# Layer 3 of a four-layer mixture-of-experts kernel: extra work moved inside a tile's slot, on ScalarE in front of the rounding, on TensorE in front of the down products

## The reference, cut to what matters

```python
# the conditioned part, for each chosen expert and the shared one
g = x @ gate_w;  u = x @ up_w
x1 = sum_e w_e * (gelu(g, approximate=True) * u) @ down_w
# the layer's own part
h   = rmsnorm(x1) * gamma1
q   = (h @ Wq + bq).reshape(b, t, 16, 16)
kv  = ((h @ Wdown + bdown) @ Wup + bup).reshape(b, t, 16, 32)   # k, v
att = softmax(einsum('bthd,btgd->bthg', q, k) / 4)              # heads against heads of one token
x2  = x1 + einsum('bthg,btgd->bthd', att, v).reshape(b, t, 256) @ Wo + bo
gate = softmax(rmsnorm(x2) * gamma2 @ Wg + bg)
out  = x_in + x2 + einsum('btd,edf,bte->btf', h2, We, gate)
```

## Time and profile before

| | us |
|---|---|
| median of 3 runs | 1460.94 (1460.05 to 1464.66) |
| the profiled execution | 1467.98 |
| its span | 1465.3 |
| TensorE busy (matmul) | 1292.0 (88%) |
| VectorE busy | 1017.1 (69%) |
| GpSimd busy | 628.9 (43%) |
| ScalarE busy | 573.3 (39%) |

### The profile page before, as it was taken

The page is one execution under the profiler, slowest core; times in us unless marked ns, Lnnn a source line. Parts: engine busy times, 40 slices in busy tenths (PEclk is TensorE's granted clock), DMA queues, the critical chain, the costliest instruction groups (busy, mean ns, idle before and its releaser), DMA issues.

```text
span 1465.3 us, 18770 instructions
## 1 busy us (share of the span) xinstructions
PE 1292.0 (88%) x6536; PEld 1093.1 (75%) x6536; DVE 1017.1 (69%) x1854; ACT 573.3 (39%) x960; POOL 628.9 (43%) x339
## 2 busy tenths in 40 slices
PE   5998999998992899838888999999899989996798
PEld 4898687897791799826677787877678777875687
DVE  8699777599662555546766433489748994799986
ACT  3401423303320688714445454434443344432242
POOL 4320115620015567573303462375445442565691
PEclk9899999899975899969999999999899999998799
DMA  6310002310007689851101647323213161232000
GB/s 193 145 37 15 29 19 82 132 29 1 0 15 254 206 274 315 264 172 43 44 0 35 223 169 250 127 73 126 111 50 109 50 244 65 73 122 101 0 1 29
DMA packets 45885, 154.96 MB, mean 106 GB/s; under 512 B 6992, under 2 KB 7776, under 8 KB 45664
## 3 DMA queue, kind: packets, MB, share of 16 engines
q1 hardware_dynamic: 38848, 136.08, 27.7%
q0 software_dynamic: 4608, 12.59, 2.6%
q10 hardware_dynamic: 2336, 5.11, 0.9%
HBM read 120.98 MB, written 32.77 MB: 105 GB/s over the span
## 4 chain that ended last, share of the span: by engine, by line
PE 57%; DVE 22%; issue 9%; POOL 5%; ACT 4%; DMA 2%; SPq 1%; DVEq 0%; ACTq 0%; POOLq 0%
PE bank L442 17%; PE bank L446 16%; PE bank L445 16%; DVE G L498 3%; DVE bank L2472 3%; DVE acc L2496 2%; DVE F L2496 2%; POOL w_lo L679 1%; POOL VW L498 1%; PE bank L1056 1%; PE bank L1228 1%; POOL xs L687 1%; PE bank L1373 1%; DVE acc L2628 1%; PE bank L928 1%
## 5 line engine op out<-in xcount | busy, mean ns | idle before, releaser
L442 PE MATMUL bank<-x_hi,w_hi 128*128 128x512 f32 (+1 forms) x560 | 218.6, 390 | 27.9 <-POOL w_lo L725 6.3
L445 PE MATMUL bank<-x_lo,w_hi 128*128 128x512 f32 (+1 forms) x560 | 212.6, 380 | 0.0
L446 PE MATMUL bank<-x_hi,w_lo 128*128 128x512 f32 (+1 forms) x560 | 212.2, 379 | 0.0
L725 POOL TENSOR_TENSOR w_lo<-raw,w_hi 128x1024 fp32r<-128x1024 f32 x36 | 89.4, 2482 | 196.1 <-ACT w_hi L1718 181.9
L442 PE MATMUL bank<-hid_hi,w_hi 128*128 128x512 f32 x328 | 133.3, 406 | 22.6 <-DVE hid_lo L2427 12.3
L442 PEld LDWEIGHTS bank<-x_hi,w_hi 128*128 128x128 f32 x560 | 110.2, 197 | 54.5 <-issue 18.5
L1819 ACT ACTIVATE hid_hi<-bank 128x512 fp32r<-128x512 f32 x96 | 57.6, 600 | 215.1 <-DVE bank L2472 215.1
L445 PE MATMUL bank<-hid_lo,w_hi 128*128 128x512 f32 x328 | 131.2, 400 | 0.0
L446 PE MATMUL bank<-hid_hi,w_lo 128*128 128x512 f32 x328 | 130.8, 399 | 0.0
L446 PEld LDWEIGHTS bank<-x_hi,w_lo 128*128 128x128 f32 x560 | 109.7, 196 | 19.2
L445 PEld LDWEIGHTS bank<-x_lo,w_hi 128*128 128x128 f32 x560 | 110.2, 197 | 17.8
(11 more groups left out here) (468 smaller groups left out, 3537.1 us busy)
## 6 DMA issues: line engine op xcount, KB each, us to landing
raw<-in_skill SPq DMA_DIRECT2D x32, 768.0 KB
raw<-in_l1e SPq DMA_DIRECT2D x20, 513.0 KB
base<-xs SPq DMA_DIRECT2D x38, 256.0 KB, 4.4
ys<-F SPq DMA_DIRECT2D x38, 256.0 KB, 4.8
VW<-in_l1e SPq DMA_DIRECT2D x18, 513.0 KB, 5.3
w_hi<-kept SPq DMA_DIRECT2D x12, 768.0 KB, 4.3
w_lo<-kept SPq DMA_DIRECT2D x12, 768.0 KB, 6.1
raw<-in_l0c SPq DMA_DIRECT2D x12, 512.0 KB
```

What stands on the lines that cost most here:

```text
L442: i = nc.tensor.matmul(out, sh, mh, start=first, stop=False)
L445: nc.tensor.matmul(out, sh, ml, start=False, stop=False)
L446: return nc.tensor.matmul(out, sl, mh, start=False, stop=last)
L725: nc.gpsimd.tensor_tensor(lo[:, UP3], src[:, UP3], hi[:, UP3].bitcast(F32), ALU.subtract).then_inc(w_up_ready.sem, 1)
```

## The change

ScalarE: a new place between a tile's gelu and its rounding. `dense_hi` of rounds 2 to 4 goes there from behind the rounding. The four passes for the norm (squares and copies, L1744 and L1746) go there from in front of the gelu of slot 2, and into slot 1. The rounding of the transposed attention output (`o3_hi`, L1777) goes there from in front of gelu, in slot 5.

TensorE: a new place between up and down products. The sums of squares (slot 2), the second pair of queries (slot 8), keys and values 1 (slot 9), the transposes (slot 5 instead of 4) and the first of two expert products of one slot (slots 13, 14, 15, 16, 18 and 20) go there. What else these functions did stays where it was. The order of VectorE, GpSimd and SyncE, the tail's order and the buffers stay too.

```diff
-            def attention3(q, i, x, y):
+            def attention3_between(q, i, x, y):
                 w = q % 2
                 if i == 2:
                     pe.wait_ge(*sq1(q, 2))
                     pe.wait_ge(*base_ready(q, 2))
                     norm_stats(x, w).then_inc(ss1.sem, 1)
+                if i == 8:
+                    pe.wait_ge(*lat_lo(q, 1))
+                    pe.wait_ge(lat_pad.sem, 3)
+                    queries(w, 1, x)
+                if i == 9:
+                    pe.wait_ge(*q3_sb(q, 2))
+                    keys_values(1, x)
...
-            def finish3(p, i, x, y):
+            def finish3_between(p, i, x, y):
                 w, last = p % 2, p == BATCH - 1
-                if i == 4:
+                if i == 5:
                     pe.wait_ge(*sum_dve(p, 16))
                     pe.wait_ge(*sum_pool(p, 16))
                     pe.wait_ge(*(x_final(1, 2) if last else n3_F(p + 1, 2)))
...
+                for j in range(1, 16):
+                    if WE_SLOT[j - 1] != i and WE_SLOT[j:j + 2] == [i, i]:
+                        experts3(p, j, (x, y)[j % 2])
...
                 for j in range(16):
-                    if WE_SLOT[j] == i:
+                    if WE_SLOT[j] == i and WE_SLOT[j:j + 2] != [i, i]:
                         experts3(p, j, (x, y)[j % 2])
...
                     l3_up(b, i)
+                    if 0 <= q:
+                        attention3_between(q, i, x, y)
+                    if 0 <= p:
+                        finish3_between(p, i, x, y)
                     if g >= 2:
                         l3_down(g - 2)
...
-            def attention3_before(q, i, x, y):
+            def attention3_between(q, i, x, y):
                 w = q % 2
-                if i == 2:
+                if i == 1:
                     act.wait_ge(*d3_step(q, TILES3))
...
                         nc.scalar.activation(gelu3[g % 2], PB[g % 2][0][:], ACT.Gelu_apprx_tanh).then_inc(g3_gelu.sem, 1)
+                    if 0 <= q < BATCH:
+                        attention3_between(q, i, x, y)
+                    if 0 <= p < BATCH:
+                        finish3_between(p, i, x, y)
+                    if next_chunk and b > 0:
+                        dense_hi(n)
+                    if b < BATCH:
                         act.wait_ge(*g3_gated(0, g + 1))
...
                         nc.scalar.activation(hid_hi[0][:, g % HID3, :], PB[g % 2][1][:], ACT.Copy).then_inc(g3_hi.sem, 1)
-                    if next_chunk and b > 0:
-                        dense_hi(n)
```

More of the change, by code:

```diff
@@ L1250, in attention3 @@
                     norm_stats(x, w).then_inc(ss1.sem, 1)
+                if i == 8:
[5 more added lines that the diff above has]
+                    keys_values(1, x)
+            def attention3(q, i, x, y):
+                w = q % 2
                 if i == 3:
@@ L1268, in attention3 @@
                 if i == 8:
-                    pe.wait_ge(*lat_lo(q, 1))
-                    pe.wait_ge(lat_pad.sem, 3)
-                    queries(w, 1, x)
                     pe.wait_ge(*q3_sb(q, 1))
@@ L1274, in attention3 @@
                 if i == 9:
-                    pe.wait_ge(*q3_sb(q, 2))
-                    keys_values(1, x)
                     pe.wait_ge(*kv3_sb(q, 1))
@@ L1292, in finish3 @@
                         mm.then_inc(o3T_ready.sem, 1)
+                for j in range(1, 16):
+                    if WE_SLOT[j - 1] != i and WE_SLOT[j:j + 2] == [i, i]:
+                        experts3(p, j, (x, y)[j % 2])
+            def finish3(p, i, x, y):
+                w, last = p % 2, p == BATCH - 1
                 if i == 6:
@@ L1429, in _ @@
             l3_down(TILES3 * BATCH - 1)
-            attention3(LQ, 2, att_x, att_y)
+            attention3_between(LQ, 2, att_x, att_y)
             attention3(LQ, 3, att_x, att_y)
@@ L1746, in attention3_before @@
                         nc.scalar.activation(base[w][:, m, :], (x, y)[m][:], ACT.Copy).then_inc(base_ready.sem, 1)
+            def attention3_before(q, i, x, y):
+                w = q % 2
                 if i == 3:
@@ L1777, in finish3_before @@
                         nc.scalar.activation(h_hi[w][:, m, :], (x, y)[m][:], ACT.Copy).then_inc(o3_hi.sem, 1)
+            def finish3_before(p, i, x, y):
+                w = p % 2
                 if i == 11:
@@ L1868, in gate_exps @@
                 nc.scalar.activation(p, logits, ACT.Exp).then_inc(l3_exp.sem, 1)
-            attention3_before(LQ, 2, mlp_x, mlp_y)
+            attention3_between(LQ, 1, mlp_x, mlp_y)
             attention3_before(LQ, 3, att_x, att_y)
@@ L1879, in _ @@
             keys_values_out(LQ, 3, mlp_x)
-            finish3_before(LP, 5, *out_bank)
+            finish3_between(LP, 5, *out_bank)
             finish3_after(LP, 7)
```

2 lines of the change are left out of this document (1 added, 1 removed).

## The result

The changed kernel takes 1469.91 us (median of 11 runs, 1466.46 to 1473.88), the kernel before beside it on the same chip 1459.27 us (11 runs, 1454.8 to 1464.66): ratio 1.0076, 95% interval [1.0058, 1.0094], or +11.1 us. The forecast was +6.1 us and slower; the sign was right and the size short by 5 us.

The account below looks back on a forecast made before the run. TensorE, nearly full on average, has the last word in slots 3 to 11, VectorE from slot 12 to the next round's slot 2. 8.2 - 4.3 - 1.4 + 3.6 + 0 = +6.1 us on 1460.94 gives 1467.0 us, range 1458.5 to 1474.

Parts of the forecast that it names:

- Slots 8 and 9: Rounds 2 to 4: queries, keys and values wait uncovered for VectorE, down products come on top; 1.36 us per slot, +8.2 us.
- Norm and transposes, round 3: Slots 1 to 5: earlier norm passes and later transposes remove TensorE waits; -4.3 us with a new low-clock stretch, -5.9 without.
- The same, round 4: Transposes' wait goes, saving 2.2 us, norm gains 0; with an even chance of a low-clock stretch, -1.4 us.
- Weights' rounding: Slots 12 to 18, rounds 3 and 4: earlier GpSimd residue makes VectorE's products wait longer; +1.8 us a round, +3.6 us.
- the walk through slot 12: Rounds 3 and 4: stepping through durations, VectorE's product waits about 1.4 us in slot 12; 5.9 us over slots 12 to 18.
- Round 2, 0: Round 2: GpSimd's work and VectorE's products fill the port before and after, so the earlier weights' rounding changes nothing, 0 us.
- Experts' order: Slots 13 to 20: first expert product before the down products is just covered; 0, up to 1 us a round if lead gone.
- 1 (relief): Rounds 3 and 4: GpSimd's residue ends before VectorE's product, 8.3 us of waits vanish; -5.8 us, 1455.1 us, chance 0.12.
- 2: Whole kernel: gains cancel losses, no new low-clock stretches and port as today; +0.1 us, 1461 us, chance 0.20.
- rival 3: Slots 8, 9, 3 and experts' firsts: new waits bring low-clock stretches, experts' lead used up; about +12, 1473 us, chance 0.13.

Follow-up runs that it names:

- queries_back: Changed kernel with the second queries and keys and values 1 put back behind the down products; ratio to the kernel before 1.0040, loop +5.9 us.
- gains_only: Kernel before with only the norm's passes and sums of squares and the transposes moved; ratio to before 0.9970, loop -5.5 us.
- slot12_only: gains_only plus the early weights' rounding in slot 12 of rounds 3 and 4 alone; ratio to before 1.0050, loop +0.6 us.
- pool_order: gains_only with GpSimd's head product before L725 in slots 12 to 17 of rounds 3 and 4, behind VectorE's in odd slots; ratio to before 1.0027.
- small_reduced: slot12_only with the gate's two small products turned into one-input reductions, its weights' normalisation left out; ratio to before 0.9971, loop -4.9 us.
- gains_round2: gains_only plus the early weights' rounding in round 2 from slot 12 on; ratios to before 0.9968 and, run again, 0.9960.
- dense_back: Changed kernel with the weights' rounding put back behind the tile's rounding; ratio to before 1.0025, loop -1.8 us.
- experts_back: Changed kernel with both expert products of a slot put back behind the down products; ratio to before 1.0091, loop +4.8 us.
- slot12_back: Changed kernel with the weights' rounding of slot 12 of rounds 3 and 4 alone put back; ratio to before 1.0012, loop -4.5 us.
- after_reduced: Changed kernel with the gate's two small products turned into reductions, its weights' normalisation left out; ratio to before 1.0034, loop 0.0 us.

## Why the prediction was right on the sign and short on the size

- **Slots 8 and 9, +8.2 us: right.** 8.15 measured, 1.36 each, with the idle times and releasers named (1.49 and 1.44 us, forecast about 1.6 and 1.5). queries_back takes them away.
- **Norm and transposes, round 3, -4.3 us with a new slow stretch, -5.9 without: mechanism right.** It came without: -5.87. The wait at the broadcast is there (2.93 us; forecast 2.5 to 3.7). In queries_back and gains_only a stretch came, and the gain was 4.3 to 4.6 us.
- **The same, round 4, -1.4 us: right to 0.9 us.** -0.54: the stretch came (+1.59) and the transposes' wait went (-2.13). The broadcast's wait was 2.17 us, a little below the 2.5 us named as the least.
- **Weights' rounding, +3.6 us: this is the term that was mis-sized.** Slots 10 to 19 hold it and the experts' order: -1.4, +6.3 and +4.5 us in the three rounds, +9.4 together, and 12.5 us in rounds 3 and 4 without the low-clock stretch that got shorter in round 4, which is more than the +8 us that the term's own range allowed. The step that failed is the walk through slot 12, "the product waits about 1.4 us in slot 12". I walked the head product and passed over the gate's two small products, at 0.16 and 0.19 us not worth a line by their length. The rule that I had used (two SBUF inputs, the first issued wins) was right and applies to them; each of them waited anew, 1.50 and 1.05 us, and the head product behind them a third time, 2.09 us: 4.6 us. slot12_only, pool_order and small_reduced show it from three sides. The rest of the walk held: in slots 12 to 18 the head products and the softmax subtraction wait 6.4 us a round in rounds 3 and 4, forecast 5.9 (its terms as written add up to 5.7), before 4.1. The product of slot 10 waits another 1.9 us, but TensorE has the last word there, and the slot is no longer for it.
- **Round 2, 0: wrong by 1.4 us in the good direction.** I had counted GpSimd's work and the products as full before and after. VectorE's waits in its products did grow, but its idle times for GpSimd's head products, 2.8 us, and the one of 1.15 us in front of the gating of slot 11 went. gains_round2 has only the 0.9 us of its odd slots' products; the idle times stay in it.
- **Experts' order, 0 and up to 1 us a round if the lead is gone: low.** It is 0 with the weights' rounding behind (dense_back). With it in front the order costs 1.6 and 2.5 us a round (experts_back): 1.3 us in slot 16, because gelu and with it L725 come later and lie beside the product, and 0.4 and 1.3 us in slot 13.
- **Low-clock stretches.** The wait of 5.94 us in slot 13 brought one in rounds 3 and 4 that no term of the sum had, and VectorE idled 1.41 and 1.23 us behind it. Another, which before had in slots 10 to 12 of round 4, was shorter after (-1.65). It hid part of the loss.
- So the total came within the range partly by luck: in rounds 3 and 4 the weights' rounding and the experts' order were 8.9 us dearer than forecast, and round 2 (-1.4), the shorter stretch (-1.65) and round 3 without a new stretch behind the broadcast (-1.6) took some of it back.
- Of the rivals, 1 (relief) shows in the softmax subtraction, 1.1 us a round, and in the odd slots' products (0.50, 0.81 and 0.74 us in round 3), but the even slots' products lose more; 2 needed slot 12 on time, and slot12_back (ratio 1.0012) comes nearest to it, though its low-clock stretches and its waits are not those of before; 3 named +12 us, near the measured +11.1. It named low-clock stretches behind the experts' firsts, and these came in rounds 3 and 4, but those in slots 8 and 9 did not, and most of the loss is VectorE's waits in slot 12, which rival 3 does not have.

## What to carry to other kernels

Before moving GpSimd work or what releases it, list every VectorE instruction with two SBUF inputs in the stretch where it will now lie, the short ones first. In these runs each of them paid the rest of a GpSimd instruction, whatever its own length, and a row of three against back-to-back GpSimd work paid three times. Where a slot is VectorE's, that goes straight to the end (slot 12); where it is TensorE's, it is free (slot 10 of round 3: the product waits 1.94 us, and the slot is as long as before). A wait for work that starts when the present one ends (slots 8 and 9) can't be hidden by more of the same queue: leave something independent between.

## What the runs showed of the hardware that I had not expected

- A VectorE product of 128x4 elements took 1.66 us beside GpSimd's subtraction, for 0.16 us alone; one of 128x32 took 1.24 and 2.34 us for 0.19. Reductions of the same size in the same place took 0.16 and 0.19 us.
- It works the other way too: beside a VectorE head product L728 took 2.29 us on GpSimd, for 1.29.
- The lower clock behind one wait showed up as an idle time of VectorE a slot later: behind TensorE's 5.94 us the granted clock was 0.50 for 2.9 us, and VectorE then idled 1.41 us.
- TensorE's idle time of 2.93 us was followed by a granted clock of 1.00 in round 3, and one of 2.17 us at the same place of round 4 by slow matmuls at 0.43 us spacing; in after_reduced 2.41 us by 1.00 and 2.32 us by 0.72. In these rows the length of the idle time does not tell which.
